# Four graph layers on one core: the order of ScalarE's round in the first attention

## The reference, cut to what matters

```python
xp = (x @ W).reshape(N, H, F)                       # H = 4, F = 32
s_src = jnp.einsum('nhf,hf->nh', xp, a_src)
s_tgt = jnp.einsum('nhf,hf->nh', xp, a_tgt)
e = _elu(s_src[src] + s_tgt[tgt], ELU_ALPHA)        # alpha 0.2
m = jax.ops.segment_max(e, tgt, num_segments=N)
m = jnp.where(jnp.isfinite(m), m, 0.0)
ex = jnp.exp(e - m[tgt])
denom = jax.ops.segment_sum(ex, tgt, num_segments=N)
alpha = ex / denom[tgt]
msg = alpha[:, :, None] * xp[src]
out = jax.ops.segment_sum(msg, tgt, num_segments=N)
```

## Time and profile before

| | us |
|---|---|
| median of 3 runs | 4807.97 (4806.36 to 4817.33) |
| the profiled execution, its own time | 4812.4 |
| its span, first to last instruction | 4810.7 |
| first gather of the first attention | starts at 1241.5 |
| last gather of the first attention | starts at 2380.6 |
| PE busy in the span | 3498.6 (73%) |
| POOL busy in the span | 3322.3 (69%) |
| DVE busy in the span | 2713.0 (56%) |
| ACT busy in the span | 1320.5 (27%) |

### The profile page before, as it was taken

The page is one execution under the profiler, slowest core; times in us unless marked ns, Lnnn a source line. Parts: engine busy times, 40 slices in busy tenths (PEclk is TensorE's granted clock), DMA queues, the critical chain, the costliest instruction groups (busy, mean ns, idle before and its releaser), DMA issues. The chain is left out here.

```text
span 4810.7 us, 82491 instructions
## 1 busy us (share of the span) xinstructions
PE 3498.6 (73%) x18822; PEld 2823.9 (59%) x18822; DVE 2713.0 (56%) x8356; ACT 1320.5 (27%) x4613; POOL 3322.3 (69%) x3348
## 2 busy tenths in 40 slices
PE   4999999998488888787738988888968333443433
PEld 2555555554377777777727878888864333333333
DVE  6677777666356556666675666666564433333332
ACT  4444444443244444444422222222212000000000
POOL 4777777775577777777507777777750777777776
PEclk8999999999555555555555555555559555555555
DMA  4555444450344343333312223332215222222222
GB/s 93 111 106 97 90 88 88 89 90 16 102 99 101 98 101 97 98 97 96 66 28 56 77 72 76 81 85 60 56 40 219 53 52 51 52 53 51 52 52 57
DMA packets 489853, 378.45 MB, mean 79 GB/s; under 512 B 307089, under 2 KB 442043, under 8 KB 486316
## 3 DMA queue, kind: packets, MB, share of 16 engines
q0 software_dynamic: 106496, 184.24, 17.1%
q1 hardware_dynamic: 383144, 192.14, 16.7%
HBM read 327.50 MB, written 33.83 MB: 75 GB/s over the span
## 5 line engine op out<-in xcount | busy, mean ns | idle before, releaser
L1054 POOL DMA_INDIRECT mlp_row<-tab,mlp_index x832 | 840.5, 1010 | 308.0 <-issue 243.0
L1054 POOL DMA_INDIRECT gat_row<-tab,gat_index x832 | 847.8, 1019 | 293.4 <-issue 224.9
L1054 POOL DMA_INDIRECT rel_row<-tab,rel_index x832 | 808.4, 972 | 255.2 <-issue 231.7
L1054 POOL DMA_INDIRECT att_row<-tab,att_index x832 | 803.6, 966 | 253.4 <-issue 249.1
L1446 PE MATMUL rel_ps_sum<-rel_row,rel_hot 128*128 128x128 f32 x1664 | 426.2, 438 | 649.3 <-DMA rel_row<-tab,rel_index 649.3
L1446 PEld LDWEIGHTS rel_ps_sum<-rel_row,rel_hot 128*128 128x128 f32 x1664 | 370.7, 328 | 705.4 <-DVE rel_hot L1471 414.1
L1676 PE MATMUL gat_ps_sum<-gat_row,gat_hot 128*128 128x136 f32 x1664 | 443.1, 448 | 179.0 <-ACT gat_sums L1625 128.5
L1872 PE MATMUL att_ps_sum<-att_row,att_hot 128*128 128x136 f32 x1664 | 446.1, 448 | 116.1 <-DVE acc L1357 112.3
L1676 PEld LDWEIGHTS gat_ps_sum<-gat_row,gat_hot 128*128 128x128 f32 x1664 | 389.1, 331 | 193.4 <-ACT gat_hot L1619 122.5
L1357 DVE TENSOR_TENSOR acc<-acc,rel_ps_sum 128x128 f32 x416 | 119.5, 287 | 666.8 <-PE rel_ps_sum L1446 637.0
L1872 PEld LDWEIGHTS att_ps_sum<-att_row,att_hot 128*128 128x128 f32 x1664 | 381.7, 326 | 191.8 <-DVE acc L1357 187.7
(11 more groups left out here) (276 smaller groups left out, 6087.0 us busy)
## 6 DMA issues: line engine op xcount, KB each, us to landing
mlp_aim<-in_dst SPq DMA_DIRECT2D x416, 128.0 KB
gat_aim<-in_dst SPq DMA_DIRECT2D x416, 128.0 KB
mlp_row<-in_edge_attr SPq DMA_DIRECT2D x416, 64.0 KB
tab<-n_stage SPq DMA_DIRECT2D x25, 1024.0 KB
mlp_row<-tab,mlp_index POOLq DMA_INDIRECT x832
gat_row<-tab,gat_index POOLq DMA_INDIRECT x832
att_row<-tab,att_index POOLq DMA_INDIRECT x832
rel_row<-tab,rel_index POOLq DMA_INDIRECT x832
```

The lines of the kernel that those rows point to most:

```text
L1054: gp.indirect_dma_start(rows[n][b][:, t, :], None, tables[n], bass.IndirectOffsetOnAxis(index[b][:, n, t:t + 1], axis=0)).then_inc(s_g[b], 16)
```

## The change

Only ACT's list of stages in the first attention differs. `lay` keeps its place and lag. `bring_tgt` and all the other stages get a lag that is larger by 4. Within a step `keep_sum`, `measure_gap` and `make_hot` now stand in front of the stages of a group, and `keep_sum` in front of the other two. The number of instructions is the same but for the pipeline's four more steps at the end, which hold no new work.

```diff
-            pipeline(act, [(0, lay), (0, bring_tgt), (4, at_end(bring_local)), (5, at_end(fifth_exp)),
-                           (6, at_end(to_lanes)), (9, at_end(weight)), (14, measure_gap), (15, make_hot), (19, keep_sum), (21, at_end(fade_exp))], WIDE)
+            pipeline(act, [(0, lay), (4, bring_tgt), (23, keep_sum), (18, measure_gap), (19, make_hot),
+                           (8, at_end(bring_local)), (9, at_end(fifth_exp)), (10, at_end(to_lanes)), (13, at_end(weight)),
+                           (25, at_end(fade_exp))], WIDE)
```

## The result

The changed kernel takes 4779.1 us (median of 4 runs, 4777.16 to 4784.31) against 4809.41 us for the kernel before (4 runs, 4806.36 to 4817.33): a ratio of 0.9936, 95% interval 0.9919 to 0.9953, or 30 us less. The forecast was 4773.

A forecast was written before the change was run, and what follows sets the result against it. A group loop through ACT's late copies of sums was taken to stall POOL's gathers. Terms -37.7 + 2 + 1.5 - 0.7 = -34.9 us gave 4773 us against the median (4777 against the profiled execution), range 4761 to 4797.

The forecast's parts named there:

- The bound and its size: POOL's idle time in front of the 832 gathers beyond its 0.306 us gap: 37.7 us to be had.
- 2 near the end: Near the stage's end, a block landing 10.6 us late uses up one group's slack: 2 us of stalls stay.
- The place of the stall and its cause: POOL at block 8n+15, once a group: waits for the sum of block 8n-1, held by ACT's late copy, not indices.
- the rival that the lead does the work: The indices' four-block lead gives the gain, not ACT's order; same time as forecast, 0.66 with either reason.
- The two sites: Copies moved in front of `weight` (2.4 us) and `to_lanes` (1.1 of 3.3 us): group loop 3.5 us shorter.
- the first site: Copy in front of `to_lanes`: sum of block 76 starts 3.3 us sooner, block 77's message leaves 1.1 up to `back`.
- The slack: POOL's own issue is late next: 2.3 us of slack at block 8n+15's gather, 1.7 for the sum of block 8n.
- every second group keeps its stall: Rival: the 1.7 us slack fails where DVE's loop turns over; half of 37.7 us won, 4789 us, chance 0.16.
- What stood behind the copy: On ACT, gap, one-hot and group stages now wait behind the copy; cost nothing, at most 2 us in 26 groups.
- slower: Rival: late PE sums delay `fifth_exp` behind the copy; 1.6 us in 26 groups, +42, 4850 us, chance 0.08.
- the stretching given back: POOL's gathers stretch as its idle time falls: 1.5 us added to their busy time, bounds 0 and 37.7.
- The tail: The 71 us without gathers, where DVE is busy 54 us and copies are hardly waited for: -0.7 us.

The follow-up runs named there:

- the order alone: ACT's new order of stages with all lags as before, against the kernel before: 4770.97 us, 0.9922; on the slower chips 5891.91 us, 0.9963.
- the kernel with the shorter gathers: ACT's new order with the old lags, and the factors that `scale` reads written into PSUM, against the kernel before: 4748.81 us, 0.9869.

## Why the prediction was right, step by step

**The bound and its size.** Right. The idle time beyond POOL's gap was to go, 37.7 us of it less 2 near the end: it went from 293.4 to 257.1 against "about 257". The two waits that are left are where the earlier trace rows put them.

**The place of the stall and its cause.** Right. The name in the page (ACT's indices) was misleading, as argued: the order alone, without any lead for the indices, removes those waits too, and leaves 8.3 us in 24 waits in their row. That refutes the rival that the lead does the work. The lead was tested by itself only on the other kind of chip (1.0018, 1.0013).

**The two sites.** In the frame of a group's landing (1716.98 before, 1710.37 after), `back` began 1743.88 - 1716.98 = 26.9 us behind it and now 1736.25 - 1710.37 = 25.9: 1.0 won, 1.1 predicted. The sum of block 79 began 33.97 us behind it and now 30.59: 3.4 won, 3.5 predicted, and the loop in the kernel with the shorter gathers says 3.4 too. The averages over groups 4 to 23 are 26.81 and 25.73 us for `back`, 33.97 and 30.43 us for the sum: 1.1 and 3.5 won, so the single group was no luck. The message of block 77 did hold back the first site, as said. PE's `back` in the kernel before:

```profile
1743.88 3.62 PE L1667 MATMUL gat_ps_back<-ident,TMP 32*128 32x32 f32 x16
```

**The slack.** The sum of block 79 begins at 1740.96, so its buffer lets a gather go 3.04 us later, as before, at 1744.00, and POOL gets to block 95 at 1746.27: 2.3 us, as predicted for this group. In other groups less is left, down to 4.17 - 3.02 = 1.15 us, which working from one group could not show. For block 80 it is 1746.84 + 3.04 = 1749.88 against 1751.27: 1.4, predicted 1.7. The rival "every second group keeps its stall" hung on that number and is refuted by the timeline, which has no such stall before 2319.99.

**What stood behind the copy.** In group 10 `fifth_exp` came 1.3 us after its input, and in no group did `elu` wait for it, as costed at nothing. The rival "slower" would have needed that wait.

**The term that was mis-sized.** Busy time of the gathers: +1.5 us predicted, +4.7 measured. In the changed execution the median gather is 947 ns in place of 944, and 832 × 3 ns are 2.5 us of it. The order alone, in an execution whose median is 944, has 849.9 us, +2.1. So the stretching given back is about 2 us and the rest is the difference of two executions, which I had no term for. The tail, costed at -0.7 with bounds 0 and -3.3, came out at -2.5 here and at -1.2 in the second execution of the changed kernel (2352.3 to 2423.2).

**How close the total was.** Partly luck. While POOL gathers the sum says 34.2 us less and 31.4 were measured; in the tail it says 0.7 and 2.5 were measured. The two misses have opposite signs, and together they give 33.9 against 34.9. The rest of the program, where the code is the same, took 5.8 us more in the changed execution; the forecast has no term for it, and it is most of what separates this execution (4784.3 us) from the 4777 forecast for it.

**What was right on this kind of chip only.** The floor of 42.6 us a group (42.9 measured, the spacing of `add_terms` from group 4 to 23) is POOL's own pace there. On the others a group takes 48.8 us with the order alone, and what sets that pace is open.

## What to carry to other kernels

On an engine that is mostly idle, order the work of a step by who waits for it: what can run while the engine would wait goes in front of the instruction that waits. Size the gain by the bottleneck's idle time beyond its own gap, not by how much the chain is shortened: here 3.4 us were taken from the loop and only about 1.4 us a group came back, because POOL's own pace was the next limit. Making the gathers themselves shorter took the kernel to 4748.8 us. And follow a wait to the instruction that could really have ended it before believing the name beside it.

## What the runs showed of the hardware that was not expected

**A gather beside `scale`.** It takes 3.05 us at 1715.71, 0.95 with the factors in PSUM at 1790.33, while `scale` takes as long as before (2.35 and 2.34 us). The long ones are not slowed in proportion, they are held: in the kernel before, in all 23 groups in which a gather is issued beside `scale`, the longest one starts at various times and ends 0.81 to 0.83 us after `scale` has ended. With the factors in PSUM no gather beside `scale` takes over 1.00 us, and over the stage the gathers are busy 48 us less. The Trainium skill says, in "GPSIMD Engine Reference" (Specifications), that GpSimd's SBUF interfaces are shared with VectorE and that there is contention with DVE instructions that have two SBUF inputs. By this rule, the trace agrees: with one of the two inputs moved to PSUM the stretching beside `scale` is gone.

**Two kinds of chip.** The same program takes 4808 to 4814 us on one kind and 5914 to 5987 on the other. On the slower kind engines stand idle where the profile names nothing that they wait for (some 20 us ahead of DVE's one-hots in straight code), and the order alone, worth 0.9922 on one, was worth 0.9963 on the other. What lies behind it is open, and so is whether it is the chip itself.

**TensorE's clock.** In the changed kernel, whose sum behind `lanes` follows with no wait, stretches at the higher of the two levels (1.2 and 2.4 GHz) are more frequent: of 194 sums that the trace of the stage shows with all eight matmuls, 13 ran in under 1.5 us instead of 2.15, seven of them in 1.19, against 1 of 194 before. With the order alone there are 9. The window is of the changed kernel, behind `lanes` of the next group, in the columns of the earlier trace rows; the line under it is one of those sums.

```profile
1763.00:1769.00 6.00, 5.57 (x34) 4.77 (x33) 4.00 (x11) 2.30 (x9) 4.78 (x5) 0.72 0.50 119
```
```profile
1766.59 1.19 PE L1677 MATMUL gat_ps_sum<-gat_row,gat_hot 128*128 128x136 f32 x8
```

The granted clock is 0.72 of full speed in these six microseconds, and 0.54 over the stage in place of 0.52. No run isolates the cause. It did not set the time: the gathers follow at POOL's own gap.
